# A graph network on one Trainium2 core: the last pass, with two row lists in byte offsets and ScalarE issuing the rows of one of them

## The reference

```python
h = x @ Wr                                   # for each of the 8 types r
s, d = h @ a_src, h @ a_dst
e = leaky_relu(s[src] + d[dst], 0.2)         # masked to the edges of type r, and the self loops
w = exp(e - segment_max(e, dst)[dst])
alpha = w / segment_sum(w, dst)[dst]
out += segment_sum(alpha[:, None] * h[src], dst) + br
```

## Time and profile before

| what | value |
|---|---|
| median of 3 runs | 8059.67 us (8032.0 to 8060.22) |
| the profiled execution | 8032.9 us |
| its span, first to last instruction | 8031.1 us |
| mean granted TensorE clock, share of full speed | 0.727 |
| busy in the span | PE 57%, DVE 56%, ACT 12%, POOL 72% |
| SP's rows in the last pass (`work<-rel_d`) | 2176 DMAs of 0.3 KB |
| POOL's gathers in the last pass (`gat<-rel_d,idx`) | 1551 |

### The profile page before, as it was taken

How to read it: one execution, slowest core, us unless ns; L and a number is a source line. 1 busy time by engine, 2 the same in 40 slices (tenths; PEclk the granted TensorE clock), 3 DMA queues, 4 the chain that set the end, 5 groups by cost and what they waited for, 6 DMA issues and landing times. The chain is left out here.

```text
span 8031.1 us, 133429 instructions
## 1 busy us (share of the span) xinstructions
PE 4542.0 (57%) x26578; PEld 3836.9 (48%) x26579; DVE 4522.3 (56%) x12211; ACT 993.3 (12%) x3180; POOL 5800.2 (72%) x6027
## 2 busy tenths in 40 slices
PE   3566566663466666665366666666613556555555
PEld 2455565553345454444244454454313555555555
DVE  4555555554556555654444554554534666666666
ACT  0000000000000000000000000000201233434333
POOL 7777777776777777777677777777267777777771
PEclk6778878786677778877577887778755666666667
DMA  2211111112322222222211111111444555555553
GB/s 64 44 36 33 35 33 36 34 35 47 69 61 62 61 62 62 61 62 55 44 33 33 33 33 34 32 34 32 132 128 111 129 144 138 146 137 142 143 142 87
DMA packets 678635, 570.23 MB, mean 71 GB/s; under 512 B 443949, under 2 KB 451931, under 8 KB 677808
## 3 DMA queue, kind: packets, MB, share of 16 engines
q1 hardware_dynamic: 430048, 295.34, 13.4%
q0 software_dynamic: 191776, 203.12, 13.0%
q10 hardware_dynamic: 55984, 63.18, 2.3%
HBM read 454.34 MB, written 100.74 MB: 69 GB/s over the span
## 5 line engine op out<-in xcount | busy, mean ns | idle before, releaser
L906 POOL DMA_INDIRECT gat<-x_d,idx x2960 | 2846.6, 962 | 956.0 <-issue 901.3
L906 POOL DMA_INDIRECT gat<-rel_d,idx x1551 | 1498.4, 966 | 633.0 <-issue 472.7
L906 POOL DMA_INDIRECT gat<-in_x,idx x1482 | 1429.6, 965 | 466.2 <-issue 451.6
L1426 PE MATMUL p_all<-oh,gat 128*128 128x256 f32 x1568 | 627.6, 570 | 797.5 <-DMA gat<-x_d,idx 757.4
L1412 PE MATMUL p_all<-oh,msg 128*66 128x128 f32 x3136 | 610.9, 377 | 778.6 <-DVE oh L1869 778.6
L1426 PE MATMUL p_all<-oh,msg 128*128 128x256 f32 x1568 | 597.9, 548 | 759.3 <-DVE oh L1869 401.3
L1412 PEld LDWEIGHTS p_all<-oh,msg 128*66 128x66 f32 x3136 | 551.3, 203 | 821.4 <-DVE msg L1995 803.2
L1426 PEld LDWEIGHTS p_all<-oh,gat 128*128 128x128 f32 x1568 | 426.5, 285 | 941.3 <-DMA gat<-x_d,idx 841.2
L1869 DVE SCALAR_TENSOR_TENSOR oh<-dstf,fine_col,p_a 128x512 f32<-128x512 f32 x1176 | 823.6, 741 | 23.7 <-DVE sum_t L1968 4.7
L1426 PEld LDWEIGHTS p_all<-oh,msg 128*128 128x128 f32 x1568 | 407.4, 272 | 885.4 <-ACT msg L1060 809.9
L1580 PE MATMUL p_b<-oh,msg 128*72 128x128 f32 x3136 | 662.1, 399 | 68.1 <-ACT msg L1169 38.5
(11 more groups left out here) (299 smaller groups left out, 6839.4 us busy)
## 6 DMA issues: line engine op xcount, KB each, us to landing
spare<-x_d SPq DMA_DIRECT2D x5888, 0.2 KB
spare<-x_d ACTq DMA_DIRECT2D x5888, 0.2 KB
he_d<-gat ACTq DMA_DIRECT2D x196, 288.0 KB
ea<-he_d SPq DMA_DIRECT2D x196, 288.0 KB
ea<-in_edge_attr SPq DMA_DIRECT2D x196, 256.0 KB
drow<-dst_d SPq DMA_DIRECT2D x196, 256.0 KB
gat<-x_d,idx POOLq DMA_INDIRECT x2960
spare<-in_x SPq DMA_DIRECT2D x2944, 0.2 KB
```

Source lines behind the costliest of these rows:

```text
L906: nc.gpsimd.indirect_dma_start(out=gat[:, q, s, :] if width == HROW else got[:, q, s, :], out_offset=None, in_=table, in_offset=bass.Indir ...
L1426: ins = nc.tensor.matmul(p_sum[:, c % 2, 0:2 * W], rows_of(s), oh[:, c % 2, s:s + 2, :].rearrange("p s w -> p (s w)"), start=(s == 0), sto ...
```

## The change

The last pass lends 40 columns in place of 17: SP those of every 7th group, range(12, 196, 7), 27 groups; and a second list, range(22, 196, 14), 13 groups, whose rows ScalarE issues and whose column SP copies. No group is in both. The numbers of all lists are multiplied by 288 on VectorE ahead of the pass, so that they are byte offsets into `rel_d`, and the row DMAs take them as such. ScalarE issues its rows at the end of each step. It waits first for the copy of the column that had the buffer before. The second side buffer lies in a free part of `trip`. SP and ScalarE wait for the multiplied lists (`s_prep`) ahead of their first step.

```diff
-LAST_SPREAD = 11
-LAST_LENT = range(LAST_SPREAD + Q + 1, G, LAST_SPREAD)
+LAST_SPREAD = [7, 14]
+LAST_LENT = [range(LAST_SPREAD[0] + Q + 1, G, LAST_SPREAD[0]), range(LAST_SPREAD[1] + Q + 4, G, LAST_SPREAD[1])]
...
-        side3 = part_of(work, 2 * BT * D, 2, HROW)
-        side3_i = toh[0:len(LAST_LENT), :, :, :].rearrange("k u s r -> k (u s r)").bitcast(i32)
+        side3 = [part_of(work, 2 * BT * D, 2, HROW), part_of(trip, 4500, 2, HROW)]
+        side3_i = [toh[32 * w:32 * w + len(LAST_LENT[w]), :, :, :].rearrange("k u s r -> k (u s r)").bitcast(i32) for w in range(2)]
...
+        def last_rows(eng, w, t):
+
+            for k, to in enumerate(LAST_LENT[w]):
+                if not to - LAST_SPREAD[w] <= t < to:
+                    continue
+                if w == 1 and k > 1 and t == to - LAST_SPREAD[w]:
+                    eng.wait_ge(s_lent[w], 16 * (3 * len(LENT[w]) + k - 1))
+                lo, hi = [4 * (P // 4 * (t - to + LAST_SPREAD[w] + j) // LAST_SPREAD[w]) for j in range(2)]
+                if lo == hi:
+                    continue
+                _, at = nc.values_load_multi_w_load_instructions(
+                    side3_i[w][k:k + 1, lo:hi], engines=[eng.engine], min_val=0, max_val=4 * HROW * (N * R - 1),
+                    skip_runtime_bounds_check_because="a source is the number of a node, a type one of R, here in bytes")
+                for p, v in zip(range(lo, hi), at):
+                    eng.dma_start(side3[w][p:p + 1, k % 2, :].bitcast(u8), rel_bytes[bass.ds(v, 4 * HROW)].unsqueeze(0))\
+                        .then_inc(s_side[w][k % 2], 16)
...
-                    for p, v in zip(range(lo, hi), row_of):
-                        sp.dma_start(side3[p:p + 1, k % 2, :], rel_d[bass.ds(v, 1), :]).then_inc(s_side[0][k % 2], 16)
...
+            def last_columns(t):
+
+                for w in range(2):
+                    if t in LAST_LENT[w]:
+                        k, q = LAST_LENT[w].index(t), t % Q
+                        sp.wait_ge(s_hest[q], 16 * (t // Q))
+                        sp.wait_ge(s_side[w][k % 2], 16 * P)
+                        sp.sem_clear(s_side[w][k % 2])
+                        sp.dma_start(gat[:, q, S - 1, :], side3[w][:, k % 2, :]).then_inc(s_lent[w], 16)
...
-                for k, t in enumerate(LAST_LENT):
-                    sp.dma_start(side3_i[k:k + 1, :], key_d[:, t, S - 1].unsqueeze(0)).then_inc(s_load[1], 16)
+                for w, k, t in [(w, k, t) for w in range(2) for k, t in enumerate(LAST_LENT[w])]:
+                    sp.dma_start(side3_i[w][k:k + 1, :], key_d[:, t, S - 1].unsqueeze(0)).then_inc(s_load[1], 16)
...
-                last_column(t + Q)
-                last_rows(t + Q)
-
-            sp.wait_ge(s_load[1], 48 + 16 * len(LAST_LENT))
+                last_columns(t + Q)
+                last_rows(sp, 0, t + Q)
+
+            sp.wait_ge(s_prep, 6)
             behind_the_gather(sp, feed)
...
                 last_layer(it, i, lo)
-
+                last_rows(act, 1, lo + Q)
+
+            act.wait_ge(s_prep, 6)
             behind_the_gather(act, store_and_weigh)
...
             layers34()
 
+            dve.wait_ge(s_load[1], 48 + 16 * sum(len(of) for of in LAST_LENT))
+            ch.start()
+            for w in range(2):
+                ch.add(vec.tensor_single_scalar(side3_i[w], side3_i[w], 4 * HROW, op=ALU.mult))
+            ch.wait()
+            dve.sem_inc(s_prep, 1)
             dve.wait_ge(s_table, 4)
```

More of the change, by code:

```diff
@@ L343, in lent @@
         def lent(n, t):
-            return any(t in of for of in LENT) if n < 3 else t in LAST_LENT
+            return any(t in of for of in LENT) if n < 3 else any(t in of for of in LAST_LENT)
         def lands(n, t):
@@ L469, in program @@
         X_bytes = [t.rearrange("n d -> (n d)").bitcast(u8) for t in X[0:3]]
+        rel_bytes = rel_d.rearrange("n d -> (n d)").bitcast(u8)
         Y = {0: x1_d, 1: x2_d, 3: x3_d, 5: out}
@@ L1151, in landed @@
                 act.wait_ge(s_gat[q], lands(3, t))
-                if t in LAST_LENT:
-                    act.wait_ge(s_lent[0], 16 * (3 * len(LENT[0]) + LAST_LENT.index(t) + 1))
+                for w in range(2):
+                    if t in LAST_LENT[w]:
+                        act.wait_ge(s_lent[w], 16 * (3 * len(LENT[w]) + LAST_LENT[w].index(t) + 1))
                 nc.scalar.activation(score[0:P, bass.ds(t + 1, 1), 0, :].rearrange("p a s -> p (a s)"),
```

## The result

The changed kernel takes 8074.07 us (median of 16 runs) against 8054.22 for the kernel before (16 runs): **1.0024 of before, 95% interval 1.0017 to 1.0032**. I had forecast 8031, 0.36% less. On the chip of a later set of runs the ratio was 1.0027 (1.0017 to 1.0036).

A forecast was written before the change was run, and what follows sets the result against it. POOL's gathers were taken to bound the last pass; 28.7 us less, all else covered, took the profiled 8032.9 us to 8004.2, and the median's 26.8 us above it gave 8031 us, range 8000 to 8072.

The forecast's parts named there:

- the gain to be had: POOL, last pass: 23 fewer gathers at 1.248 us each, 28.7 us less, only while POOL stays the bound.
- 0.43 us are left: SP's step: +1.53 us against 2.12 us of waiting, less 0.16 for the shorter step, leaves 0.43 us.
- the wait on ScalarE's rows: SP at 13 columns: waits for rows ScalarE issued one step before; costs nothing until ScalarE is a step late.
- the 4.29 that I put on it: ScalarE, 182 steps: one load and 9.14 rows cost 4.29 us per step, between nothing and 5.08.
- rival 2: End of ScalarE's steps: ScalarE becomes the bound, rows at 5.08 us per step, +149 us, 8209 us; chance 0.10.
- none is absorbed: ScalarE: none of its 1.32 us per group of other waits vanishes, so it needs 10.03 us per group.
- Rival 1: ScalarE's late copy delays VectorE and the gain is eaten: 10.03 us per group against 10.00, 8065 us; chance 0.21.
- The ring of copy, look and drow: Argument for the gain being eaten: three engines wait for each other through copy, look, drow and reload.
- The drain: After the last gather: 199 us left, taken to move with the last group's landing and stay near 199 us.
- a growing drain: Sign of a wrong forecast, after the last gather: VectorE and TensorE left behind while POOL ran on; no size given.
- Rival 3: SP and ScalarE hinder each other when issuing: 1.99 us per step on SP, +255 us, 8315 us; chance 0.03.
- Preload, multiplication and slots: Start of second pass +15.0 us, list multiplication about 0.6 us: both covered, the latter by POOL's four slots.

The follow-up runs named there:

- every 12th group on SP: Changed kernel with SP's list at every 12th group instead of every 7th, ScalarE's list unchanged: 0.9982 of before, 14.5 us less.
- SP's fixed addresses: Changed kernel with SP's rows read from fixed addresses, no numbers loaded into registers for them: 0.9972 of before.
- the second trace of before: The kernel before, with no edit, traced once more: span 8034.2 us.
- the lists exchanged: Changed kernel with SP taking every 14th group and ScalarE every 7th, 39 columns: 1.0114 of before, 92 us slower.
- the version with every 8th group: Changed kernel with SP at every 8th group, ScalarE every 14th, column copied one step later, 36 columns: 0.9976 of before.
- ScalarE's fixed addresses: Changed kernel with ScalarE's rows read from fixed addresses without register loads, SP's rows as in the change: 1.0004 of before.
- SP's list alone: Changed kernel with SP at every 7th group, 27 columns, and no rows on ScalarE: 0.9994 of before.
- the second trace of the change: The changed kernel run and traced again, on the chip of a later set of runs: 1.0027 of before.

## Why the prediction was wrong

**What bounded the kernel, and the gain to be had: right.** The gathers went down by 23 at their old price. When SP was relieved, the pass from first to last gather became 31 us shorter, and with every 12th group on SP the 11 gathers brought 14.5 us for 13.7 worked out.

**The step that failed is SP's.** "0.43 us are left" was to leave POOL the bound; nothing was left. In the steady stretch of the changed kernel a step of SP takes 10.29 us (the mean of 133 steps from index to index in its timeline), where POOL's pace without waits would be 9.84 by the prediction; with SP's fixed addresses, where POOL is the bound, a step takes 9.95. Against the second trace of before (136 steps, 6385 to 7765):

```text
us per step          before (again)  change   more   predicted
rows                     4.79         6.02    1.23     1.12
load ahead of rows       1.24         1.77    0.53     0.35
column copy              0.04         0.10    0.06     0.06
gap ahead of a column    0.03         0.26    0.23     0
other issues and gaps    1.74         1.79    0.05     0
gap ahead of drow        2.24         0.35   -1.89
whole step              10.08        10.29    0.21
```

The two large terms were priced low. What the rows add came out a tenth higher, at 0.329 us each and not 0.318, and what the load adds by half: about half of the loads take what the slope says (1.20 us for 16 numbers, 1.43 for 20), but the others take longer, up to 3.0 us, and the means are 1.51 and 1.72. And one was costed at nothing: at every second of its columns SP now waits about 3 us (29.4 us, 12 times) for the rows it has issued itself one step earlier. I had named the wait on ScalarE's rows there and not the one on SP's own. The sum is 2.10 us more per step instead of 1.53.

That wait belongs to a place in the cycle of 14 groups. In nine traces, the second of before, both of the change and six of the runs, every wait there of 1.5 us or more falls at the column of a group that is 5 past a multiple of 14. With the lists exchanged, where SP stands 614.9 us waiting for VectorE, these columns still wait 2.2 to 4.0 us in the steady stretch. One step earlier, ahead of the last rows, SP issues two tables that take 7.4 and 9.5 us to land; that the rows land behind them fits, but is not shown. A list of every 11th group has one such column in the whole pass, a list of every 7th group has one at every second column.

**The margin itself was read wrongly too.** I set a mean need against a mean pace. In the change, SP's step without the gaps ahead of a column and of drow takes 9.69 us, below 9.84. But these two gaps remain, 0.60 us per step: the 0.26 at its columns, and the wait for VectorE of up to 7.8 us, ten times in the stretch (the 32.7 us above), about once in each 14 groups. In 11 of the 14 steps of that cycle the gap ahead of drow is 0.05 us, in two some 0.25, in one 3.58: the mean is mostly the room of a single step. In the version with every 8th group, where the gain does come through, SP has 8.71 us of work per step and 1.20 us ahead of drow.

**ScalarE: the price was right in size, the place of it was not.** A load takes 0.83 us in the mean and a row some 0.4 us, 4.4 us per step for the 4.29 that I put on it. Of these, 225.4 / 135 = 1.67 us show as time in which the engine stands for issuing; the rest runs beside activations or beside its waits. So rival 2 did not come about. But "none is absorbed" of rival 1 is what happened: ScalarE's waits for others grew, from 34.5 to 400.2 us for reloads alone, because SP was late. Rival 1 had the right outcome, 8065 against 8074, with the wrong engine: the gain was eaten on SP's queue. The 16 us that ScalarE's fixed addresses gave back sit there too, in the loads ahead of SP's rows; what lengthens these is not shown. The ring of copy, look and drow that rival 1 named shows in the run with the lists exchanged, where ScalarE is the late one.

**The drain** did not simply move with the last gather. From ScalarE's last copy to the end it is 182 to 188 us in all traces; what grows is the time from the start of the last gather to that copy: 12.6 us in the second trace of before, 21.0 with SP's list alone, 25.7 in the change. The prediction had named a growing drain as a sign that other engines had been left behind, and that is what it was; it holds 13 us of the change's loss.

**Rival 3** (locked issuing) is not borne out: a row on SP takes 0.331 us without rows on ScalarE and 0.329 with them. In the steady stretch of the change, 1048 of SP's row DMAs run at the same time as one of ScalarE's and 1420 don't; the median is 228 ns for both. The Trainium skill (Perfetto Trace Analysis, "DMA Instruction — HWDGE") puts the wait for the lock inside the reported duration of a DMA. By that, a lock between the two queues would show in these rows, and none does.

**Preload, multiplication and slots** cost nothing visible: the second pass shows no new wait of POOL, and the first gather of the last pass is at 5859.3 us in the second trace of the change, 5866.2 in that of before.

## What to carry to other kernels

Before work is moved to a queue, sum up its step with every wait that the moved work makes for itself, and compare it not with the mean time that the queue waits but with what is left when the waits that come in lumps are taken off. Ask too at which steps of a longer cycle the moved work falls: here every second of SP's columns came at a step where its rows had not landed. A shared load is best set a step below the point where the mean still fits: with the column copied one step later in both, 36 columns brought 19 us and 40 lost 6 (the interval of the 40 holds no change as well). And when a run adds an instruction whose result nobody uses, look for it in the trace before its time is read.

## What was not expected of the hardware

A row DMA takes 0.41 us of SP's time when its address is worked out from an index and 0.33 when the register already holds the byte offset; with a fixed address and no register it still takes 0.308, of which the DMA is 252 ns. So most of the cost is the DMA itself, where the prediction had put what lies beyond 228 ns down to the making of the address.

ScalarE's queue issues rows beside running activations: with fixed addresses one row of 0.27 us for about each activation of 0.33. There 79% of the rows run beside an activation for over half of their time. With register addresses it is 43% in the change and 12% with 18.3 rows a step, and these 18.3 rows made ScalarE the bound of the whole kernel.
